# Attention's position tables by row bands, its first near terms by two engines, first biases copied on chip, and the feed-forward's loads on three queues

## What is computed

```
x = x + 0.5 * switch_ffn(ln(x))      # 8 experts of 128 -> 512 -> 128, gelu, top-1
x = x + relative_attention(ln(x))    # 16 heads of 8
x = x + 0.5 * switch_ffn(ln(x))      # the same weights
x = x + 0.5 * spline_ffn(ln(x))
x = x + causal_softplus_attention(ln(x))
x = x + 0.5 * spline_ffn(ln(x))
```

```
q, k, v  = heads(h @ Wq + bq), heads(h @ Wk + bk), heads(h @ Wv + bv)
pos_k    = heads(rel_embeddings @ Wk + bk)              # 64 positions
c2p[i,j] = q[i] . pos_k[clip(rel(i,j) + 32)]            # rel: log buckets of i - j
p2c[i,j] = k[j] . pos_k[clip(-rel(i,j) + 32)]
probs    = softmax((q @ k.T + c2p + p2c) / sqrt(24))
out      = layernorm(probs @ v @ Wo + bo + h)
```

## Time and profile before

| what | us |
|---|---|
| runs of the kernel before | 755.36, 753.46, 753.55 (median 753.55) |
| span of the profiled execution | 752.3 |
| median less that span | 1.25 |
| busy PE, DVE, ACT, POOL | 581.5, 532.0, 453.5, 203.6 |
| first feed-forward up to its first slot | 37.1 |
| its slots up to the start of the last | 77.5 |
| from there to the attention's start | 16.9 |
| attention up to the first bias addition | 35.0 |
| its 64 quads and the end of the last | 288.6 |
| the other four parts | 297.2 |

### The profile page before, as it was taken

The page is one execution under the profiler, slowest core; times in us unless marked ns, Lnnn a source line. Parts: engine busy times, 40 slices in busy tenths (PEclk is TensorE's granted clock), DMA queues, the critical chain, the costliest instruction groups (busy, mean ns, idle before and its releaser), DMA issues. The chain is left out here.

```text
span 752.3 us, 17249 instructions
## 1 busy us (share of the span) xinstructions
PE 581.5 (77%) x5361; PEld 417.1 (55%) x5361; DVE 532.0 (71%) x1881; ACT 453.5 (60%) x983; POOL 203.6 (27%) x262
## 2 busy tenths in 40 slices
PE   4399993079999999999899998452996673678780
PEld 3288883045666666767576766341985342346450
DVE  7543320967787788999799995873224799867897
ACT  3245562047888888999799996550552534376723
POOL 1745332401912720660400000043443200211200
PEclk9999998589999999999999999655998787799985
DMA  8878567699899999999744421833554000000001
GB/s 241 221 240 289 181 215 205 212 300 331 242 349 330 296 313 309 255 251 345 185 136 141 134 65 22 238 86 127 170 180 121 2 1 0 0 1 1 1 1 56
DMA packets 130378, 127.80 MB, mean 170 GB/s; under 512 B 27962, under 2 KB 108002, under 8 KB 129394
## 3 DMA queue, kind: packets, MB, share of 16 engines
q1 hardware_dynamic: 122722, 99.85, 46.7%
q0 software_dynamic: 3920, 25.26, 8.8%
q10 hardware_dynamic: 3648, 1.59, 0.8%
HBM read 68.37 MB, written 48.79 MB: 156 GB/s over the span
## 5 line engine op out<-in xcount | busy, mean ns | idle before, releaser
L1714 DVE CUSTOM_DVE_ANT_0 l0am_prob<-l0am_ps_s,l0am_bias 128x512 f32<-128x512 f32 x256 | 166.6, 689 | 33.8 <-PE l0am_ps_s L1788 24.1
L1631 ACT ACTIVATE l0am_prob<-l0am_prob,l0am_neg_top 128x512 f32<-128x512 f32 x256 | 171.4, 723 | 6.8 <-DVE l0am_neg_top L1714 6.8
L1801 PE MATMUL l0am_ps_t<-c_ident,l0am_prob 128*128 128x128 f32 x1024 | 129.0, 275 | 0.4 <-DVE l0am_probT L1701 0.4
L1801 PEld LDWEIGHTS l0am_ps_t<-c_ident,l0am_prob 128*128 128x128 f32 x1024 | 110.9, 141 | 16.5 <-issue 8.0
L636 ACT ACTIVATE l0f_h<-l0f_psU,l0f_experts 128x128 f32<-128x128 f32 x212 | 60.7, 369 | 83.0 <-PE l0f_psU L962 82.9
L829 DVE COPY l0f_xsT<-l0f_psT 128x128 f32<-128x128 f32 x53 | 15.4, 291 | 99.0 <-PE l0f_psT L952 99.0
L1701 DVE COPY l0am_probT<-l0am_ps_t 128x512 f32<-128x512 f32 x128 | 82.2, 684 | 1.4 <-PE l0am_ps_t L1801 1.4
L1788 PE MATMUL l0am_ps_s<-l0am_ks,l0am_qs 32*128 32x512 f32 x512 | 74.4, 651 | 3.5 <-DVE l0am_neg_top L1714 2.6
L1625 ACT COPY l0am_probT<-l0am_ps_t 128x512 f32<-128x512 f32 x128 | 68.5, 589 | 10.7 <-PE l0am_ps_t L1801 10.7
L531 POOL DMA_INDIRECT token_results<-l0f_ys,l0f_token_i x53 | 51.1, 965 | 78.3 <-DVE l0f_ys L839 75.0
L1815 PE MATMUL l0am_ps_cg<-l0am_probT,l0am_v 128*9 128x128 f32 x2048 | 68.7, 275 | 2.7 <-DVE l0a_heads L1725 2.7
(11 more groups left out here) (340 smaller groups left out, 949.6 us busy)
## 6 DMA issues: line engine op xcount, KB each, us to landing
l0am_bias<-near_terms SPq DMA_DIRECT2D x128, 192.0 KB, 4.6
near_terms<-l0am_near POOLq DMA_DIRECT2D x6, 3072.0 KB, 12.3
l0f_mine<-l0f_experts SPq DMA_DIRECT2D x53, 256.0 KB, 2.4
near_terms<-l0am_near SPq DMA_DIRECT2D x4, 1536.0 KB, 7.5
l0o_rows_k<-position_k SPq DMA_DIRECT2D x12, 512.0 KB, 6.9
l0f_experts<-in_L_ffn_w SPq DMA_DIRECT2D x2, 2048.0 KB
l0f_experts<-in_L_ffn_w SPq DMA_DIRECT2D x16, 256.0 KB
position_q<-l0o_rows SPq DMA_DIRECT2D x16, 256.0 KB, 4.3
```

What stands on the lines that cost most here:

```text
L1631: nc.scalar.activation(prob[:, k, :], prob[:, k, :], ACT.Exp, bias=neg_top[:, k:k + 1], scale=-1.0)\
L1714: dve.tensor_tensor_reduce(out=prob[:, k, :], in0=ps_s[:, j, :], in1=bias[:, j, at:at + S], scale=-1.0, scalar=HUGE, op0=ALU.add, op1=ALU.min,
L1801: last = pe.transpose(ps_t[:, BANK_OF[j], i, :], prob[:, u % SLOTS_, i * P:(i + 1) * P], ident[:, :])
```

## The change

**The start.** SP keeps the first biases and first matrices; POOL loads the eight second matrices and their biases before its scatters; ACT loads the attention's constants between two exponentials. SP stores four of the blanks, ACT the other four. `place_slots(0)` moves ahead of `choose(1)`. SP and PE no longer wait for all weights together.

**The tables.** `wext` is gone, and with it `extend`, its copies and 18 of the 20 bias matmuls. q and k of a batch are projected (slots 22 and 23), kept as they are (`qk`) and stored as the stacked rows; a table quarter is then a matmul of a 32-row band of `spread` (positions of four heads) with the same 32 rows of q or k, two bands at a time in two parts of the array (slots 24 to 27), one copied by ACT and one by DVE. Rows are loaded in 8 DMAs rather than 32.

**Around the attention's start.** The feed-forward ends without draining POOL; who needs its results waits for them in the attention. Only batch 0's values are made before the first quad. Of batch 0's 32 bands DVE adds 21 and POOL 11; POOL then scales and adds the feed-forward's results of batches 2 and 3. ACT fills `bias` with zeros. The first group's bias goes from `near` straight into `bias`, in 32 DMAs that each read one partition (28 by SP, 4 by ACT). The other groups' near terms are stored by POOL, four DMAs of 8 partitions for a group.

**In the quads.** Turn, projection, tables and values of batches 1 to 3 go into 20 quads, 0 to 5, 7 to 13 and 17 to 23 (`LATE_STEPS`); the statistics of batches 2 and 3 into quads 3 to 6, with their normalised tokens by POOL. DVE copies its two heads in one instruction, and divides one quad later.

```diff
             def _(sp):
-                for e in range(EXPERTS):
-                    sp.dma_start(experts[:, e, SLAB_W2:SLAB_B2].rearrange("p (k d) -> p k d", k=FC),
-                                 w["w2"][e].rearrange("(k p) d -> p k d", p=P)).then_inc(weights_in, 16)
-                if aside:
-                    aside.load(sp)
...
-                sp.wait_ge(weights_in, FFN_LOADS * 16)
-                sp.wait_ge(b1_ready, 1)
+                if opening:
+                    sp.wait_ge(blanks_ready, 1)
+                    for e in range(EARLY_BLANKS):
+                        store_blank(sp, 0, e, blanked[e])
+                sp.wait_ge(up_weights_in, 16)
                 sp.wait_ge(rows_ready, 1)
...
             def _(pool):
+                if opening:
+                    load_down_weights(pool)
...
             def _(act):
                     exponentials(2)
+                    aside.load(act)
                     exponentials(3)
...
             def _(dve):
                     count_slots(0)
+                    place_slots(0)
                     choose(1)
                     prepare(3)
                     rank(1)
                     shift(2)
-                    place_slots(0)
...
+    def multiply(self, pe, cn, banks):
+        b, i = divmod(cn, BATCH_ROWS)
+        side, first = divmod(i, QUARTERS)
+        pe.wait_ge((self.q_ready, self.k_ready)[side], b + 1)
+        for n, bank in enumerate(banks):
+            r = slice(32 * (first + n), 32 * (first + n) + 32)
+            pe.matmul(bank, self.aside.spread[r, side, :], self.qk[r, side, :], start=True, stop=True,
+                      tile_position=(32 * (first + n), 0)).then_inc(self.tab_psum, 1)
...
+            def first_bias(queue, t, halves):
+                for s in halves:
+                    for j in range(GROUP):
+                        p, at = NB * GROUPS * j + 2 * t + s, NEAR_AT[t] + 64 * s
+                        queue.dma_start(bias[64 * s:64 * s + 64, j, at:at + WIN],
+                                        near[p:p + 1, :].rearrange("p (q w) -> p q w", w=WIN)).then_inc(bias_in[t], 16)
...
+                def store_near(b, g):
+                    part = 64 * WIN
+                    for j in range(GROUP):
+                        p = NB * (GROUPS * j + g)
+                        pool.dma_start(bass.AP(dram["near"].tensor, (b * P + p) * part, [(part, NB), (1, part)]),
+                                       near[p:p + NB, :]).then_inc(near_out[g], 16)
...
+                near_bands(pool, FIRST_POOL_RUNS).then_inc(near_pool, 1)
+                opening.scale_results(pool, 2)
+                opening.scale_results(pool, 3).then_inc(scaled, 1)
+                pool.wait_ge(scaled, 1)
+                opening.add_scaled(pool, 2).then_inc(added, 1)
+                opening.add_scaled(pool, 3).then_inc(added, 1)
...
+LATE_STEPS = {0: [("turn", 1), ("project", 1)], 5: [("values", 1)],
+              7: [("turn", 2)], 8: [("project", 2)], 13: [("values", 2)],
+              17: [("turn", 3)], 18: [("project", 3)], 23: [("values", 3)]}
+LATE_STEPS |= {first + n: [("rows", BATCH_ROWS * b + 2 * n)] for b, first in ((1, 1), (2, 9), (3, 19)) for n in range(QUARTERS)}
```

More of the change, by code:

```diff
@@ L1162, in copy_bias, with multiply_bias @@
+                n0 += n
+        last.then_inc(self.spread_ready, 1)
+    def multiply_bias(self, pe):
+        pe.wait_ge(self.spread_ready, 1)
+        for side in range(2):
+            last = pe.matmul(self.ps[:, 0, side * QUARTERS:(side + 1) * QUARTERS], self.spread[:, side, :], self.less_near[:, :],
+                             start=True, stop=True)
+        last.then_inc(self.bias_psum, 1)
     def copy_bias(self, act):
         act.wait_ge(self.bias_psum, 1)
-        self.nc.scalar.copy(self.row_bias[:, :], self.ps[:, 0, 0:BATCH_CHUNKS]).then_inc(self.wext_ready, 1)
@@ L1418, in near_build @@
                     view(rows_k, RIGHT_ROW * NARROW + c0 - NARROW_AT[RIGHT_ROW], (0, 16), (1, WIN - c0)), ALU.add)
-            between(last)
-            for pair in range(TABLE_CHUNKS):
-                if pair:
-                    arrived(pair)
-                for d0, d1, pq, _ in RUNS_OF[pair]:
-                    at, width, r = 64 - d1, d1 - d0 + 1, ROW_OF[pq]
-                    last = engine.tensor_tensor(
-                        view(near, at, (WIN + 1, 64), (1, width)), view(rows_q, r * 64, (1, 64), (0, width)),
-                        view(rows_k, r * NARROW + at - NARROW_AT[r], (1, 64), (1, width)), ALU.add)
@@ L1428, in near_build, with near_bands @@
-            return last
-        with nc.Block() as block:
+            return last
+        def near_bands(engine, runs):
+            for d0, d1, pq, _ in runs:
+                at, width, r = 64 - d1, d1 - d0 + 1, ROW_OF[pq]
+                last = engine.tensor_tensor(
+                    view(near, at, (WIN + 1, 64), (1, width)), view(rows_q, r * 64, (1, 64), (0, width)),
+                    view(rows_k, r * NARROW + at - NARROW_AT[r], (1, 64), (1, width)), ALU.add)
+            return last
@@ L1532, in _ @@
[L1532 to L1551 removed]
+                            wait_stack(b)
@@ L1564, in _ @@
                 last.then_inc(near_cleared, 1)
-                pool.memset(bias[:, :, :], 0.0).then_inc(filled, 1)
-                steps = 0
-                def between(last):
-                    nonlocal steps
-                    steps += 1
-                    last.then_inc(near_steps, 1)
-                    pool.wait_ge(near_steps, steps)
+                pool.wait_ge(near_cleared, 1)
+                pool.wait_ge(near_corner, 1)
+                for pair in FIRST_BY_POOL:
+                    rows_arrived(pool, 0, pair)
@@ new lines, in wait_late_copies @@
+                def wait_late_copies(pe, q, by_act):
+                    for kind, what in LATE_STEPS.get(q, ()):
+                        if kind == "turn" and not by_act:
+                            pe.wait_ge(xT_ready, what + 1)
+                        elif kind == "project":
+                            pe.wait_ge(*((opening.q_ready, what + 1) if by_act else (opening.k_ready, what + 1)))
+                        elif kind == "rows":
+                            pe.wait_ge(opening.rows_by_act if by_act else opening.rows_by_dve, what // 2 + 1)
+                        elif kind == "values" and not by_act:
+                            pe.wait_ge(v_ready, what + 1)
```

812 lines of the change are left out of this document (403 added, 409 removed).

## The result

The changed kernel took **1020.7 us** (median of 1020.28, 1025.48 and 1021.12, with 1011.0 for the profiled execution), the kernel before 753.5 beside it: a ratio of 1.352 with an interval of 1.346 to 1.358. Forecast were 733.0 us and a range of 718 to 746. The sign was wrong.

The account below looks back on a forecast made before the run. PE was taken to bound the slot loop and quads, chains of waits the stretch between; 752.3 - 0.3 - 6.9 - 9.0 - 7.8 + 3.4 = 731.7, plus 1.3 outside the span, gave 733.0 us, range 718 to 746.

Parts of the forecast that it names:

- Slower: Rival, quads: POOL's 8-partition stores use few DMA engines and set the pace, 66 us on, 799 us; chance 0.05.
- 30 us a group: Within the slower rival: time of a group's stores through two DMA engines, where four plain quads last 16.7 us.
- some five groups: Within the slower rival: groups not covered by a batch's head start, each paying 13.3 us, 66 us on.
- 4.7 us of DVE beside the first biases' DMAs: Prelude, after near: DVE's work for batch 1's tokens beside the bias DMAs, 4.7 us, then the first addition at 142.5.
- The quads, 3.4 on: Attention's quads: moved-in work adds 4.2 us, stalls give back 0.8, so 3.4 us longer.
- The term for stalls: Quads: 3.0 us of stall expected, for 3.8 in the kernel before.
- Late rows or biases: Rival: last rows' landing or quad 16's biases come some 7 us late, 740 us; chance 0.20.
- SP's queue is lighter: Argument used against the rival of late rows or biases, which put the time at 740 us; chance 0.20.
- Near, 22.0 by alternation: Prelude: DVE and POOL take turns rather than overlap, 3.0 + 7.1 + 6.6 + 5.3 = 22.0 us, near ready at 138.2.
- side by side: Rival, near: DVE and POOL overlap, first addition at 131, 11 us less, 722 us; chance 0.15.
- To the attention, 9.0 off: From last slot to attention's start: fewer row loads, span shrinks from 16.9 to 7.9 us, 9.0 less.
- The start, 0.3 off: Before the first slot: SP no longer waits for the first biases' copy; slot starts at 36.8, 0.3 us earlier.
- The loop, 6.9 off: Loop of slots: cheaper extend and bias slots, six product slots for eight; 6.9 us less.

Follow-up runs that it names:

- e1: Changed kernel, but all four groups of batch 0 stored and whole batches awaited; each store still reads 8 neighbouring partitions: 1039.5 us (one run).
- e2: As e1, but the 8 partitions of a store lie 4 apart, in SBUF and in DRAM: 863.1 us, ratio 1.145 to the kernel before.
- e4: Changed kernel, but POOL stores nothing until all 32 first-bias copies have landed: 1046.5 us (one run).
- e12: Changed kernel with 128-partition, 12 KB stores, batches 2 and 3 paced, another partition order, DVE alone on bands, batch 0's stores held for tiles 0 and 1: 791.5 us.
- e14: e12 with the first group's bias loaded through DRAM like all the others, without the 32 one-partition copies: 786.3 us, ratio 1.045 to the kernel before.
- e6: e5 with all 32 bands of batch 0 added by DVE alone: 843.4 us, ratio 1.117 to the kernel before.
- e5: Changed kernel with partitions reordered so that a group's store reads 32 neighbours in one DMA: 846.4 us, ratio 1.124 to the kernel before.

## Why the prediction was wrong

- **The step that failed** is the dismissal of the rival *Slower*, "a POOL store of 8 partitions of 48 KB spreads over few DMA engines", at a chance of 0.05; with it the sum put POOL's stores at nothing. The place was right and the mechanism was not. I argued only over the engines and let the rival fall when the packets turned out to be spread over them; that the source lies in few neighbouring partitions I did not look at. e1 and e2 show that this alone is worth 176 us. Its price, 30 us a group, was of the right order (20.2 measured in batch 1), but I let "some five groups" pay it; in fact each batch's stores hold the quads up for 63 to 75 us, and SP's loads with them (keys after 75 us), which no step had.
- The nearest row seemed to speak for it: a store of 32 partitions landed in 7.5 us, and one of 8 with a quarter of the bytes was taken as a quarter of the work. But those 32 partitions lie 4 apart, over all of SBUF, and the 8 are neighbours. The rule on the number of engines that was weighed beside it (the Trainium skill, DMA: Bandwidth & Descriptors, "How many engines (k)") takes the sizes of the outer dimensions and says nothing of where in SBUF the partitions lie; the measurement decides.
- **First biases, "4.7 us of DVE beside the first biases' DMAs"**: mis-sized in both conditions. With POOL's stores beside, the first addition came 57.6 us after `near`; with none, 15.6 (e4); with another order of partitions and DVE alone, still 10.2 (e12: bands end at 132.57, addition at 142.78). The forecast's own terms, 138.2 and 4.7, give 142.9 and not the 142.5 that it used.
- **The quads, 3.4 on**: the engines' part held. Without a stall, two quads with bands are 5.4 us apart (253.82, 259.19, 264.59 on PE) for 5.47 forecast, and plain ones 4.16 (693.96, 698.12) for 4.17. The term for stalls was 3.0, and PE's idle time 220. The rival *Late rows or biases* was weighed with "SP's queue is lighter"; e14 moves as many bytes in the quads as the kernel before, and its loads of keys cost PE 26.7 us.
- **Near, 22.0 by alternation**: the time was right by luck, 138.1 for 138.2. DVE began the corners at 119.99 where rows in place at 116.2 were forecast, and `near` took 18.1 us from there. Alternation held in kind: DVE's 21 bands took 15.07 where they would take 7.1 alone, so the rival *side by side* falls. But DVE stood still for 8.0 us (15.07 less 7.1), not for the 11.9 of POOL's 6.6 and 5.3. And the consequence was not drawn: DVE alone, 10.35, was better (e6).
- **To the attention, 9.0 off**: 9.0. **The start, 0.3 off**: 1.2.
- **The loop, 6.9 off**: 3.9. A product slot is 3.15 us on PE (93.06, 96.21, 99.36), not the 2.75 of the earlier trace rows; six of them are 2.4 of the missing 3.0.

## What to carry to other kernels

Before a transfer out of SBUF is cut into pieces, count which partitions each piece reads at a time: the same bytes from eight neighbours held the DMA engines 2.4 times as long as from eight that lay 4 apart, and pieces of all 128 partitions were best here, whatever their length. When an older transfer is taken as the price of a new one, compare the partitions and not only their number. Price a slow transfer not by its own landing but by what else lands late beside it: here the loads on SP's queue were slow as long as POOL's stores were out. A time that comes out right is checked by its terms: `near` was ready on time by two errors. A fresh rival is dropped only when every resource of the transfer has been looked at, not when one has.

## What was not expected of the hardware

- The dependence on the partitions itself: 97 engine-us a MB from 8 neighbours (e1), 71 from 32 (e5), 41 from 8 that lie 4 apart (e2), 37.5 from 32 that lie 4 apart (the kernel before).
- SP's loads can come far later than their own length while stores from POOL are out: a 256 KB load of keys reached PE 75 us after its issue (the changed kernel), two issues took 14.86 us (e14).
- Pieces of 3, 12 and 24 KB a partition gave the same time within 1% (812.9, 807.3, 810.7).
- Two engines adding bands from the same tiles were slower than one: 15.07 us for 21 bands beside POOL, 10.35 for all 32 alone.
